# Attention of a vision tower: scores two steps ahead, filling work over six steps, stacks by way of device memory

## The reference

```python
h = _L0_tok_ref(x, W, b)
h = h + _L0_attn_ref(_layernorm(h), qkv_w, qkv_b, ln_g, ln_b)
h = h + _L0_ffn_ref(_layernorm(h), W1, b1, W2, b2, ...)
...
attn = jnp.einsum('bhnd,bhmd->bhnm', q, k) * D ** (-0.5)
neigh = lax.conv_general_dilated(attn, kernel, ...)
attn = attn - BETA * neigh
attn = softmax(attn - max(attn)); out = attn @ v
```

## Time and profile before

| | |
|---|---|
| median of 3 runs | 2232.3 us |
| lowest run | 2219.14 us |
| profiled execution | 2232.05 us |
| its span | 2230.3 us |
| mean granted clock of PE | 0.909 |
| PE, DVE, ACT, POOL busy, share of the span | 86%, 65%, 57%, 52% |
| attention | from the start to about 1260 us |
| one pair in the middle of it | 36.2 us |

### The profile page before, as it was taken

How to read it: one execution, slowest core, us unless ns; L and a number is a source line. 1 busy time by engine, 2 the same in 40 slices (tenths; PEclk the granted TensorE clock), 3 DMA queues, 4 the chain that set the end, 5 groups by cost and what they waited for, 6 DMA issues and landing times. The chain is left out here.

```text
span 2230.3 us, 54487 instructions
## 1 busy us (share of the span) xinstructions
PE 1912.0 (86%) x17949; PEld 1428.4 (64%) x17949; DVE 1456.4 (65%) x4652; ACT 1271.6 (57%) x2469; POOL 1151.6 (52%) x1069
## 2 busy tenths in 40 slices
PE   4748888888889889888988478999999999999991
PEld 3536666666666667666766356777777777767771
DVE  4657788788878888787887435555555555564440
ACT  3547787778778787778787423433443443333330
POOL 3334545455545555454543254666666666654452
PEclk7878999899989999999998658999999999999996
DMA  3474556565656565655655226878877787798886
GB/s 108 87 182 115 123 150 132 139 135 141 150 124 158 120 163 118 154 121 148 130 143 119 70 79 189 201 190 206 184 203 183 202 197 188 196 201 177 177 178 189
DMA packets 356573, 344.07 MB, mean 154 GB/s; under 512 B 146580, under 2 KB 328144, under 8 KB 352144
## 3 DMA queue, kind: packets, MB, share of 16 engines
q1 hardware_dynamic: 314768, 300.14, 53.9%
q0 software_dynamic: 41664, 42.12, 10.9%
HBM read 175.03 MB, written 96.92 MB: 122 GB/s over the span
## 5 line engine op out<-in xcount | busy, mean ns | idle before, releaser
L1830 ACT ACTIVATE mh<-mid_bank 128x512 bf16<-128x512 f32 x336 | 201.0, 598 | 476.6 <-PE mid_bank L1521 353.4
L1742 DVE SCALAR_TENSOR_TENSOR ml<-mid_bank,mh 128x512 bf16<-128x512 f32 x336 | 231.8, 690 | 353.5 <-ACT mh L1830 343.3
L816 DVE TENSOR_REDUCE row_max<-s_bank 98x2 f32<-98x392 f32 x768 | 396.9, 559 | 96.2 <-PE s_bank L599 93.6
L1012 ACT ACTIVATE probs<-t_bank 98x392 f32<-98x392 f32 x768 | 340.9, 497 | 45.0 <-PE t_bank L615 33.3
L1896 POOL DMA_INDIRECT sums<-y_out,tail x168 | 265.2, 1578 | 177.2 <-DVE y_out L1772 121.9
L1535 PE MATMUL y_bank<-wst,mh 128*128 128x192 bf16 x1344 | 329.9, 245 | 12.2 <-DVE y_out L1772 11.7
L1538 PE MATMUL y_bank<-wst,ml 128*128 128x192 bf16 x1344 | 330.1, 246 | 0.0
L1537 PE MATMUL y_bank<-wst,mh 128*128 128x192 bf16 x1344 | 329.8, 245 | 0.0
L1185 POOL TENSOR_TENSOR x_lo<-x_buf,x_hi 128x588 f16<-128x588 f32 x128 | 186.6, 1463 | 208.7 <-ACT x_hi L993 166.3
L615 PE MATMUL t_bank<-q_stack,k_stack 104*98 104x196 f16 x1536 | 254.9, 277 | 33.4 <-ACT probs L1012 18.9
L1881 POOL DMA_INDIRECT slots<-row_r,spot x196 | 191.2, 976 | 97.3 <-issue 56.7
(11 more groups left out here) (236 smaller groups left out, 4562.5 us busy)
## 6 DMA issues: line engine op xcount, KB each, us to landing
wst<-packed SPq DMA_DIRECT2D x56, 1584.0 KB
x_buf<-in_x_t SPq DMA_DIRECT2D x32, 1176.0 KB, 7.6
q_stack<-qk_hi SPq DMA_DIRECT2D x256, 73.5 KB, 2.5
k_stack<-qk_hi SPq DMA_DIRECT2D x256, 73.5 KB, 2.5
sums<-h_buf SPq DMA_DIRECT2D x32, 294.0 KB
q_stack<-qk_lo SPq DMA_DIRECT2D x128, 73.5 KB, 2.5
k_stack<-qk_lo SPq DMA_DIRECT2D x128, 73.5 KB, 2.6
h_in<-sums SPq DMA_DIRECT2D x32, 294.0 KB
```

Source lines behind the costliest of these rows:

```text
L816: nc.vector.reduce_max(row_max[st.odd][:, :, hh:hh + 1], s_bank[hh % 2][0:HALF, :, 0:TOKENS], AX.X).then_inc(max_ready, 1)
L1012: nc.scalar.activation(probs[st.odd][:, hh], t_bank[hh % 2][0:HALF, :, 0:TOKENS], ACT.Exp).then_inc(probs_ready, 1)
L1742: nc.vector.scalar_tensor_tensor(ml[n % MID][:], mid_bank[n % MID_PS][:], 0.0, mh[n % MID][:], ALU.max, ALU.subtract).then_inc(ml_ready, 1)
```

## The change

- **Look-ahead of two.** PE computes in step s the scores of s + 2 (`LOOK`), and DVE reduces and splits their maxima; the transposes of the maxima stay one step ahead (s + 1), and all else stays where it was. The first scores of the next pair now stand at k = 4. `run_bodies` begins two steps early and writes out one more body.
- **Filling work over six steps.** On PE `before_max` and `after_max` become `between_heads` (ahead of the second half of scores_less_max) and `after_heads`. Patches move from k = 1, 2 to k = 0, 1, 2, v to k = 3, 4, ahead of the second half. On ACT and POOL the patches of the pair three ahead begin at k = 4. On ACT the copy of the max rows moves up, right behind the last exponentials; `high_rows` and `low_rows` move to k = 2, one pair later. On DVE both `take_v` move to k = 4.
- **Stacks.** `qk_hi` and `qk_lo` are stored whole, 588 KB each, in a tensor `stack_parts` in device memory (k = 1 and k = 2). When a store has landed, SP loads blocks of 32 partitions and 294 KB from it into the stacks: four from the high part (k = 2), two from the low part (k = 3).
- **x** is loaded three pairs ahead, before `blank_memory` in the first body; rows for the router go out at k = 4.
- **Filling the pipeline.** The second pair's patches and casts move up between the steps of the first pair on PE, ACT, POOL and DVE.

```diff
-DRAIN = STEPS + 1
+DRAIN = 2 * STEPS - 1
+LOOK = 2
...
-    step(0, -1)
+    for kk in range(-LOOK, 0):
+        step(0, kk)
     for body in range(2):
         for kk in range(BODY_STEPS):
             step(body, kk)
-    with eng.Fori(2, BODIES - 1) as body:
+    with eng.Fori(2, BODIES - 2) as body:
         for kk in range(BODY_STEPS):
             step(body, kk)
+    for kk in range(BODY_STEPS):
+        step(BODIES - 2, kk)
     for kk in range(BODY_STEPS + DRAIN):
         step(BODIES - 1, kk)
...
-        STACKED = 16 * 3 * HG
-
+        STACKED = 16 * 3
...
-            def stack(pr):
-
-                if pr.there:
-                    for part, plain_ready, tilde_ready, uses in (
-                            (qk_hi, plain_hi_ready, tilde_hi_ready, ((0, 0), (0, 2), (1, 0), (1, 1))),
-                            (qk_lo, plain_lo_ready, tilde_lo_ready, ((0, 1), (1, 2)))):
-                        sp.wait_ge(plain_ready, pr.u + 1)
-                        sp.wait_ge(tilde_ready, pr.u + 1)
-                        for which, r in uses:
-                            dst = (q_stack, k_stack)[which][pr.q]
-                            for hh in range(HG):
-                                at = which * HI + hh * HEAD_DIM
-                                sp.dma_start(dst[32 * r:32 * r + 32, hh::HG, :],
-                                             part[at:at + HEAD_DIM].rearrange("p r (g i) n -> p r g (i n)", i=PAIR)
-                                             ).then_inc((q_stacked, k_stacked)[which], 16)
+            def store_parts(pr, low):
+
+                if pr.there:
+                    sp.wait_ge((plain_hi_ready, plain_lo_ready)[low], pr.u + 1)
+                    sp.wait_ge((tilde_hi_ready, tilde_lo_ready)[low], pr.u + 1)
+                    sp.dma_start(stack_parts[low], (qk_hi, qk_lo)[low][:].rearrange("p r b n -> p (r b n)")
+                                 ).then_inc(parts_stored[low], 16)
+
+            def stack(pr, low):
+
+                if pr.there:
+                    sp.wait_ge(parts_stored[low], 16 * (pr.u + 1))
+                    for which, r in (((0, 0), (0, 2), (1, 0), (1, 1)), ((0, 1), (1, 2)))[low]:
+                        src = stack_parts[low, which * HI:(which + 1) * HI].rearrange(
+                            "(h p) (r g n) -> p r g h n", h=HG, r=2, g=GROUPS)
+                        sp.dma_start((q_stack, k_stack)[which][pr.q][32 * r:32 * r + 32], src
+                                     ).then_inc((q_stacked, k_stacked)[which], 16)
...
                 elif k == 0:
-                    load_x(Pair(body, kk, 2))
+                    load_x(Pair(body, kk, 3))
                     load_h(Pair(body, kk, -1))
-                    store_rows(Pair(body, kk, -2))
                 elif k == 1:
                     if kk == 1 and not (isinstance(body, int) and body == 0):
                         store_part(body - 1)
                     elif kk == BODY_STEPS + 1:
                         store_part(body)
-                    stack(Pair(body, kk, 1))
+                    store_parts(Pair(body, kk, 1), 0)
+                elif k == 2:
+                    store_parts(Pair(body, kk, 1), 1)
+                    stack(Pair(body, kk, 1), 0)
                 elif k == 3:
+                    stack(Pair(body, kk, 1), 1)
                     store_y(Pair(body, kk, -1))
                 elif k == 4:
                     store_h(Pair(body, kk, 2))
+                    store_rows(Pair(body, kk, -2))
                 if kk == 3 and isinstance(body, int) and body == 0:
...
-            def before_max(body, kk):
+            def between_heads(body, kk):
 
                 k = kk % STEPS
-                if k in (1, 2):
-                    project_patches(Pair(body, kk, 2), k - 1, 0)
-                elif k == 3:
-                    project_v(Pair(body, kk, 1), 0, (0, 1))
+                if k in (0, 1):
+                    project_patches(Pair(body, kk, 2), 0, k)
+                elif k == 2:
+                    project_patches(Pair(body, kk, 2), 1, 0, range(PCH // 2, PCH))
+                elif k in (3, 4):
+                    project_v(Pair(body, kk, 1), k - 3, (0, 1))
+
+            def after_heads(body, kk):
+
+                k = kk % STEPS
+                if k == 1:
+                    project_patches(Pair(body, kk, 2), 1, 0, range(PCH // 2))
+                elif k == 2:
+                    project_patches(Pair(body, kk, 2), 1, 1)
                 elif k == 4:
-                    project_v(Pair(body, kk, 1), 1, (1,))
                     transpose_xn(Pair(body, kk, 2), 0)
-                elif k == 5:
-                    project_qk(Pair(body, kk, 2), 0)
-                    project_qk(Pair(body, kk, 2), 1)
-
-            def after_max(body, kk):
-
-                k = kk % STEPS
-                if k in (1, 2):
-                    project_patches(Pair(body, kk, 2), k - 1, 1)
-                elif k == 3:
-                    project_v(Pair(body, kk, 1), 1, (0,))
-                elif k == 4:
                     transpose_xn(Pair(body, kk, 2), 1)
                 elif k == 5:
-                    project_qk(Pair(body, kk, 2), 2)
+                    for i in range(BLOCKS):
+                        project_qk(Pair(body, kk, 2), i)
...
-                scores(Step(body, kk, 1), (0, 1))
+                scores(Step(body, kk, LOOK), (0, 1))
                 mix(Step(body, kk, -1))
                 transpose_back(Step(body, kk, -2))
                 scores_less_max(Step(body, kk, 0), (0, 1))
-                scores(Step(body, kk, 1), (2, 3))
+                scores(Step(body, kk, LOOK), (2, 3))
+                if kk >= 0:
+                    between_heads(body, kk)
                 scores_less_max(Step(body, kk, 0), (2, 3))
-                if kk >= 0:
-                    before_max(body, kk)
                 transpose_max(Step(body, kk, 1))
                 if kk >= 0:
-                    after_max(body, kk)
+                    after_heads(body, kk)
...
-                row_maxima(Step(body, kk, 1), (0, 1))
+                row_maxima(Step(body, kk, LOOK), (0, 1))
                 normalise(Step(body, kk, -2))
...
-                        statistics(Pair(body, kk, 2), 1)
+                        take_h(Pair(body, kk, 2), 1)
+                    elif k == 4:
+                        take_v(Pair(body, kk, 1), 0)
+                        take_v(Pair(body, kk, 1), 1)
                     elif k == 5:
                         split_low(Pair(body, kk, 2))
-                row_maxima(Step(body, kk, 1), (2, 3))
-                split_maxima(Step(body, kk, 1))
+                row_maxima(Step(body, kk, LOOK), (2, 3))
+                split_maxima(Step(body, kk, LOOK))
                 if kk >= 0:
                     if k == 0:
                         add_tilde(Pair(body, kk, 1))
                     elif k == 1:
                         take_low_tilde(Pair(body, kk, 1))
                     elif k == 2:
+                        statistics_n(Pair(body, kk, -1))
+                    elif k == 3:
...
-                if kk >= 0 and k < 2:
-                    high_patches(Pair(body, kk, 2), 2 * k)
+                if k >= 4:
+                    high_patches(Pair(body, kk, 3), k - 4)
+                elif k < 2:
+                    high_patches(Pair(body, kk, 2), 2 + k)
+                elif k == 2:
+                    high_rows(Pair(body, kk, -2))
                 exponentials(Step(body, kk, 0), (2, 3))
+                copy_max_rows(Step(body, kk, 1))
                 if kk >= 0:
                     if k == 0:
                         take_high_plain(Pair(body, kk, 1))
                     elif k == 1:
                         take_high_tilde(Pair(body, kk, 1))
-                    elif k == 5:
-                        take_qk(Pair(body, kk, 2), 0)
-                        take_qk(Pair(body, kk, 2), 1)
-                    if k == 3:
+                    elif k == 3:
                         layernorm_n(Pair(body, kk, -1))
-                    elif k == 4:
-                        high_rows(Pair(body, kk, -1))
-                copy_max_rows(Step(body, kk, 1))
-                if kk >= 0:
-                    if k < 2:
-                        high_patches(Pair(body, kk, 2), 2 * k + 1)
                     elif k == 4:
                         take_xt_b(Pair(body, kk, 2))
                         split_high(Pair(body, kk, 2))
+                    elif k == 5:
+                        for i in range(BLOCKS):
+                            take_qk(Pair(body, kk, 2), i)
                     if kk in (8, 10):
...
+    stack_parts = nc.dram_tensor("stack_parts", (2, P, 2 * BLOCKS * COLS), F16).ap()
```

142 lines of the change are left out of this document (82 added, 60 removed).

## The result

The changed kernel took 2359.8 us in the median of 4 runs (2355.5 to 2363.8), beside 2229.6 for the kernel before: ratio 1.06, 95% interval 1.0553 to 1.0647. It is slower, by 130 us, and lies above my range of 2125 to 2310. The last rows of attention leave ACT at 1399.5 us instead of 1268.9, so all of it is in attention.

The account below looks back on a forecast made before the run. Attention's pairs were taken as bound by PE's hand-over waits and a nearly as late stack chain. From 2232 us, one-time gains of -34 and +3 for the pairs gave 2201 us, range 2125 to 2310.

Parts of the forecast that it names:

- What bounds the kernel now: Attention's 36.2 us pairs: a chain of hand-overs that PE waits on, and the stacks' chain with 0.4 us of slack.
- The form of the sum: A pair cannot be shorter than first scores of k = 4 to next tilde end, plus tilde end to last stack landing.
- T: The end of the tilde part of qk_hi on ACT, from which the stacks' round trip is counted.
- L = 12.7 us, from R = 255 GB/s: Time from T to the last stack's landing: 4.9 us fixed plus 2.0 MB at the assumed load rate of 255 GB/s.
- The rule of ports: Skill rule: 32 partitions reach eight ports, about 218 GB/s; landing after 14.1 us, time some 2243 us; 0.14 of the chance.
- 23.6 us from the scores of k = 4 to the next T: Work from the next pair's first scores to the next tilde end, taken as 23.6 us against 24.1 before.
- Maxima, max rows' copy and exponentials, -2 us per pair: PE's waits in attention: 1.7 us for maxima, most of 0.6 for the copy, nothing booked for exponentials; pair 34.2 us.
- One-time gains, -34 us: Load of x before blanking -23.8 us, filling of the pipeline -11, the end +1.
- A: Rival: stacks arrive in time, rate over about 330 GB/s, PE's other waits set the pair; 2145 us, chance 0.36.
- D: Rival: look-ahead shortens nothing since DVE sets its step, only one-time gains stay; 2198 us, sharing the forecast's chance of 0.42.
- C: Rival: the round trip is the new bound, PE waiting at the first scores of k = 4; 2295 us, chance 0.22.
- wrong in kind above 38: Sign that the forecast is wrong in kind: the pair rises above 38 us, against 36.3 forecast.

Follow-up runs that it names:

- e15: Changed kernel with the heads of a stack in another order, so a load's pieces are 2352 B instead of 784 B: 2322.6 us, ratio 1.0501.
- e16: e14 with the loads of weights one step later, behind the last stack load on SP: 2168.1 us, ratio 0.979 to the kernel before.
- e5: Changed kernel with stack transfers for the first two pairs only and DVE's statistics of h back in their old place: 2204.7 us, ratio 0.9891.
- e9: Changed kernel, all transfers, DVE's statistics back, POOL's split at k = 1 behind the plain low part, its sum of rows at k = 2: 2361.2 us, ratio 1.059.
- e3: Changed kernel with stack stores and loads for the first two pairs only, later scores using these stacks: 2255.6 us, ratio 1.0176.
- e13: e9 with plain halves of the stacks sent and fetched ahead of the tilde halves, whole-row stores, loads in 2352 B pieces: 2209.9 us, ratio 0.9981.
- e14: e13 with DVE's tilde low part after the first two row maxima of k = 2 instead of before them: 2205.4 us, ratio 0.9959.
- e17: e13 with each load into 16 partitions side by side instead of every second one of 32: 2358.6 us, ratio 1.0648.
- e7: e3 with DVE's statistics back in their old place and POOL's work of k = 1 behind DVE's plain low part: 2209.0 us, ratio 0.9912.
- e4: Kernel before with its 24 stack transfers for the first two pairs only, later pairs using these stacks: 2187.8 us, ratio 0.987.

## Why the prediction was wrong

*What bounds the kernel now*: right, both chains, and so was "looking further ahead would gain nothing without a faster way for the stacks". The slack of 0.4 us was the number to trust.

*The form of the sum*, pair = (first scores of k = 4 to the next T) + L: right. PE waited for the last stack in every one of the 17 pairs, so the two terms are the pair. Both were mis-sized, and these are the steps that failed.

*L = 12.7 us, from R = 255 GB/s*: 14.6 and 16.3 in turn, 15.4 on average. The fixed 4.9 us were nearly right: with 205 GB/s the same formula gives 14.7, and 0.7 us stay unexplained. R was taken between two bounds, nearer to the upper ones, which I had picked by their size of piece, and e15 shows that the size of piece was not the thing. The rule of ports, weighed at 14.1 us and 0.14 of the chance, was the one to take, though with the 23.6 below it still gives 2243 us. Averaging out the loads of weights did no harm: they stand in front of the last two loads and cost their pair 1.7 us, where 0.38 MB at 205 GB/s are 1.9.

*23.6 us from the scores of k = 4 to the next T*: 25.9, with 24.1 before. I had let the long step k = 5 give back 1.7 us. It does (6.7 us for 8.6), but k = 4 now takes 7.5 us for 5.0, most of it at the lower clock behind the stall that the late stack makes. In e16, with short stalls and the clock at 0.97, it is 24.9. Together, 2.7 + 2.3 us make the pair 36.3 + 5.0 = 41.3.

*Maxima, max rows' copy and exponentials, -2 us per pair*: each wait went as said, none of it reached the time. "If nothing else comes up" covered the late statistics (2.8% in e5, hidden behind the round trip in e9) and DVE's longer chain at k = 1, which I had booked at nothing: I had followed the moved steps on PE, ACT and SP, but not who waits for DVE's statistics.

*One-time gains, -34 us*: by the second T the changed kernel is 22.5 us ahead (120.17 for 142.63), after one pair that already costs it some 5 us. The wait of 23.8 us for x is gone; 6.4 us remain in all. The first scores come at 59.5 us instead of 69.1. So about -28: close. Missed here were the short waits for x, some 33 us in all (57.2 less 23.8), which the change took away as well; they add nothing to the time where the stack's chain, and not the load of x, sets the pair.

*The rivals*: A fell. D is half right: with the transfers left out or out of the way it is DVE's row maxima that PE waits for (49.1 us in 750 in e3, 61.2 in e13); but in the changed kernel DVE is not the bound, and e13, at 0.998, misses D's 0.985. C was right in mechanism and place; its price, 2321 us at the far end, fell short by 39 us, since it carried the same 23.6; its L of 16.7 was even too long. Its mark, "over 4 us per pair", is met (82.4 us in 19 pairs, 4.3), and so is "wrong in kind above 38".

## What to carry to other kernels

Work out the length of a loop as a closed chain (hand-over, transfer, wait, work up to the next hand-over) and take slack in it seriously: with 0.4 us of slack, a step that moves a due time forward must shorten the transfer by as much first. For a transfer's rate, look at rows that reach as many partitions, not at rows with pieces of the same size. A stall of PE may be paid twice: here the step behind it ran at a clock of 0.52 and took 7.5 us for 5.0, though no run separates the two. And a wait that leaves the list of waits has only moved if another chain is nearly as long, as e9 and e14 show from both sides.

## What the runs showed of the hardware

Loads from device memory at full DMA share moved 190 to 213 GB/s into 32 partitions, in pieces of 784 B and of 2352 B alike, and 103 to 118 into 16 side by side (e17); loads into 16 that are every second one of 32 moved 216 to 226 at a share of 0.8 (e13); a store from all 128 partitions, 376. For the partitions side by side the Trainium skill states this in "SBUF — State Buffer" (Door 1: The DMA port swizzle), 218 and 109 GB/s for eight and four ports; the runs agree within 13%. A store whose outermost dimension was 4 ran at a share of 0.27. A DVE operation that began beside a busy POOL took 4.23 us in one pair and 2.83 in the next, instead of 1.38. In the first it ended 1.24 us after POOL's second operation, in the next 1.25 us after POOL's first (711.70 + 1.81); there POOL's x_lo had its turn behind it and took 2.45 us instead of 1.30:

```profile
711.93 2.83 DVE L946 TENSOR_TENSOR qk_lo<-padded,qk_hi 128x1176 f16<-128x1176 f32 x1 [0.39 <-ACT qk_hi L1104]
```

```profile
711.70 1.81 POOL L1233 TENSOR_TENSOR att<-att,h_in 98x768 f32<-98x768 f32 x1 [0.53 <-DVE att L876]
713.47 2.45 POOL L1218 TENSOR_TENSOR x_lo<-x_buf,x_hi 128x588 f16<-128x588 f32 x1
```

What stays open: why DVE's two operations at k = 1 together cost PE 2.3 us at k = 2 in the new order and nothing in the old one was not taken further than e14; what else makes the new order 1.3 us per pair longer than the old one once the statistics are back (36.6 in e7, 35.3 in e4); and no run separates what the clock alone takes from what the wait takes.
